# Cross-attention kernel: the normalised context turned by VectorE and put in place by small transfers instead of transposed by TensorE

## What is computed

```
for layer in 1, 2:
    h   = layer_norm(x)
    qh  = (h @ wq + bq) in 16 heads of 128
    kh, vh = (context @ wk + bk), (context @ wv + bv), each with one extra bias row
    ctx = softmax(qh kh^T / sqrt(128)) vh          (per batch and head, over 1501 keys)
    x   = x + ctx @ wo + bo
x = x + gelu(layer_norm(x) @ w_fc1 + b_fc1) @ w_fc2 + b_fc2
```

## Time and profile before

| | us |
|---|---|
| median of 3 runs | 1282.16 |
| lowest, highest of them | 1279.06, 2014.25 |
| the profiled execution, its own time | 1280.71 |
| its span in the trace | 1278.9 |
| mean granted clock of TensorE | 0.996 |

### The profile page before, as it was taken

How to read it: one execution, slowest core, us unless ns; L and a number is a source line. 1 busy time by engine, 2 the same in 40 slices (tenths; PEclk the granted TensorE clock), 3 DMA queues, 4 the chain that set the end, 5 groups by cost and what they waited for, 6 DMA issues and landing times.

```text
span 1278.9 us, 26549 instructions
## 1 busy us (share of the span) xinstructions
PE 1252.2 (98%) x8140; PEld 1152.3 (90%) x8140; DVE 794.6 (62%) x1369; ACT 807.2 (63%) x1585; POOL 905.1 (71%) x750
## 2 busy tenths in 40 slices
PE   6999999999999999999999999999999999999998
PEld 6779999999999999998887999999999999999897
DVE  5745656566666666566785656666656666655654
ACT  4745666666656566676584656666666666666755
POOL 4737777777777777678673768686868686866882
PEclk9999999999999999999999999999999999999999
DMA  5401111111111111012331111111111111101131
GB/s 166 144 10 49 37 61 36 60 36 60 36 60 36 60 37 59 31 39 83 121 126 40 38 38 61 36 60 36 60 36 60 36 60 37 60 30 52 50 95 40
DMA packets 30670, 72.58 MB, mean 57 GB/s; under 512 B 3104, under 2 KB 4512, under 8 KB 30624
## 3 DMA queue, kind: packets, MB, share of 16 engines
q1 hardware_dynamic: 30336, 71.49, 18.1%
q10 hardware_dynamic: 288, 0.52, 0.1%
HBM read 71.52 MB, written 0.48 MB: 56 GB/s over the span
## 4 chain that ended last, share of the span: by engine, by line
PE 91%; DVE 4%; ACT 2%; issue 2%; DMA 0%; POOL 0%; DVEq 0%; ACTq 0%; SPq 0%; POOLq 0%
PE psum L682 36%; PE psum L703 13%; PE psum L704 13%; PE psum L705 13%; PE psum L650 5%; PE psum L747 4%; PE psum L714 2%; PE psum L671 2%; DVE g_prod L1193 1%; PE psum L689 1%; PE psum L696 1%; PE psum L600 1%; DVE qh L1222 1%; ACT on L994 1%; DMA w_raw<-weights 0%
## 5 line engine op out<-in xcount | busy, mean ns | idle before, releaser
L509 POOL TENSOR_TENSOR pt<-slots,pt 125x512 fp32r<-125x512 f32 (+1 forms) x384 | 446.4, 1168 | 216.5 <-ACT slots L988 184.9
L682 PE MATMUL psum<-qs,ctx 128*125 128x384 f32 (+1 forms) x2304 | 543.1, 372 | 1.3 <-ACT slots L1019 0.8
L682 PEld LDWEIGHTS psum<-qs,ctx 128*125 128x125 f32 x2304 | 396.4, 187 | 47.5 <-ACT slots L1019 8.3
L703 PE MATMUL psum<-ctx,pt 125*128 125x258 f32 x1344 | 385.5, 287 | 2.8 <-ACT on L994 2.7
L704 PE MATMUL psum<-ctx,pt 125*128 125x256 f32 x1344 | 379.3, 282 | 0.0
L705 PE MATMUL psum<-ctx,pt 125*128 125x258 f32 x1344 | 379.1, 282 | 0.0
L1281 DVE TENSOR_TENSOR t_max<-psum,t_max 125x512 f32<-125x512 f32 (+1 forms) x320 | 199.2, 622 | 261.2 <-PE psum L682 260.9
L987 ACT ACTIVATE pt<-slots 125x512 fp32r<-125x512 f32 (+1 forms) x384 | 221.1, 576 | 193.1 <-DVE slots L1269 178.6
L1019 ACT ACTIVATE slots<-psum 125x512 f32<-125x512 f32 (+1 forms) x384 | 207.0, 540 | 141.8 <-DVE t_max L1281 132.2
L703 PEld LDWEIGHTS psum<-ctx,pt 125*128 125x128 f32 x1344 | 253.4, 189 | 19.9 <-ACT on L994 12.7
L704 PEld LDWEIGHTS psum<-ctx,pt 125*128 125x128 f32 x1344 | 254.1, 189 | 6.0
(11 more groups left out here) (104 smaller groups left out, 1062.2 us busy)
## 6 DMA issues: line engine op xcount, KB each, us to landing
nat_stage<-ctx_nat SPq DMA_DIRECT2D x64, 375.0 KB
tr_stage<-ctx_tr SPq DMA_DIRECT2D x64, 375.0 KB, 3.0
w_raw<-weights SPq DMA_DIRECT2D x70, 256.0 KB, 2.7
dk_rest<-dk_rows SPq DMA_DIRECT2D x2, 768.0 KB, 6.3
w_raw<-weights ACTq DMA_DIRECT2D x2, 256.0 KB, 4.2
dk_first<-dk_rows SPq DMA_DIRECT2D x2, 256.0 KB, 4.5
xres<-x_rows SPq DMA_DIRECT2D x4, 112.0 KB, 4.3
out_rows<-xres SPq DMA_DIRECT2D x4, 112.0 KB, 1.9
```

Source lines behind the costliest of these rows:

```text
L509: nc.gpsimd.tensor_tensor(split_weights(h, LO, c), slot(h, c), as_f32(split_weights(h, HI, c)), ALU.subtract).then_inc(pt_lo, 1)
L682: last = mm(scores(h, k), ctx_tr_chunk(half, a, c), qs[h][:, m, half, 0:R], start=(half, a, m) == terms[0], stop=(half, a, m) == terms[-1])
L703: mm(out_bank[:, 0:D + 2], hi, ctx_nat_hi(c), start=(c == 0), stop=False, skip_group_check=True)
```

## The change

`on` of a group is no longer transposed by TensorE. VectorE transposes it in blocks of 32 x 32 into a tile `turn` (one instruction a group, at step c = 7). `turn` then holds every block turned in itself, but in the partitions of its rows. 16 DMA transfers a group, one for each pair of a quarter of the rows and a quarter of the dimensions, issued from SyncE's queue, take the blocks to their partitions in `qt`. Each covers 32 partitions and, in each, 8 (h = 0) or 6 (h = 1) runs of 32 elements, 128 bytes. The last group of a layer is still transposed by TensorE.

`qt` is stored by tile: tile, then half, then row. Its readers and writers take the new strides. `turn` lies over `dk_first` and `g_prod`, so the load of `dk_first` for the second layer moves behind the last move of the first layer. `EARLY` is now 49 tiles, so the late copies of heads 0 and 1 cover 7 tiles instead of 3. In SyncE's queue, the moves of a batch's first group stand between tr 0 and nat 1, those of its second group between tr 1 and nat 0; those of the last batch's first group stand behind the first four weight loads of the output stage.

```diff
+QUARTER, QUARTERS = 32, 4
+MOVES = QUARTERS * QUARTERS
+TURNED = GROUPS - 1
+TURN_STEP = 7
+EARLY = NT - TILES
 NAT_W = 2 * D + 2
...
-        qt = sb("qt", [P, DC, B, FLAT], F32)
+        qt = sb("qt", [P, NT, DC, P], F32)
...
+        at_turn = place_at[0]
         dk_first = sb("dk_first", [P, 4 * K], F32)
         g_prod = [sb(f"g_prod{s}", [P, DC, K], F32) for s in range(2)]
+        assert place_at[0] - at_turn == GT[0] * D * 4
...
+        place_at[0] = at_turn
+        turn = sb("turn", [P, GT[0], D], F32)
...
-        qt_flat = qt[:].rearrange("p c b f -> p c (b f)")
+        qt_tiles = qt[:].rearrange("p n c r -> p c n r")
 
         def head_rows_of(h):
 
-            return qt[:].rearrange("p c b (t h e) -> p c (b t) h e", h=H, e=TQ)[:, :, :, ds(h, 1)].rearrange(
+            return qt[:].rearrange("p n c (h e) -> p c n h e", h=H, e=TQ)[:, :, :, ds(h, 1)].rearrange(
                 "p c n a e -> p c n (a e)")
+
+        def of_tiles(ap):
+
+            return ap.rearrange("p (n r) -> p n r", r=P)
 
...
+                def move_context(b, h):
+
+                    sp.wait_ge(turned, INIT + l * TURNED + b * 2 + (h + 1))
+                    settle(sp)
+                    for rows in range(QUARTERS):
+                        for dims in range(QUARTERS):
+                            source = turn[rows * QUARTER:(rows + 1) * QUARTER, 0:GT[h]].rearrange(
+                                "p j (c q r) -> p j c q r", c=DC, q=QUARTERS)[:, :, :, dims].rearrange(
+                                "p j c r -> p (j c) r")
+                            goal = qt[dims * QUARTER:(dims + 1) * QUARTER,
+                                      ds(b * TILES + h * GT[0], GT[h])].rearrange(
+                                "p n c (q r) -> p n c q r", q=QUARTERS)[:, :, :, rows].rearrange(
+                                "p n c r -> p (n c) r")
+                            sp.dma_start(goal, source).then_inc(moved, 16)
+
                 def batch_loads(b, first, last):
 
                     nat, tr = l * (B * PIECES) + b * PIECES, l * (B * PIECES) + b * PIECES + PIECES
                     if not last:
                         load_tr(b + 1, tr, 0)
                     if not first:
+                        move_context(b - 1, 0)
                         for p in range(1, PIECES):
                             load_nat(b, nat + p, p)
                     if not last:
                         load_tr(b + 1, tr + 1, 1)
+                    if not first:
+                        move_context(b - 1, 1)
+                    if not last:
                         load_nat(b + 1, nat + PIECES, 0)
                         for p in range(2, PIECES):
                             load_tr(b + 1, tr + p, p)
 
                 load_bias(l)
-                if l + 1 < LAYERS:
-                    load_dk_first(l + 1)
                 batch_loads(0, True, False)
                 with sp.Fori(1, B - 1) as b:
                     batch_loads(b, False, False)
@@ -423,6 +454,10 @@
                 settle(sp)
                 for u in range(4):
                     load_weight(l * JOBS + (H + u), u, l * H + (H - 3 + u))
+                move_context(B - 1, 0)
+                if l + 1 < LAYERS:
+                    sp.wait_ge(moved, INIT + (l + 1) * (TURNED * MOVES * 16))
+                    load_dk_first(l + 1)
...
-                src = qt_flat[:, half, ds(b * FLAT + h * GT[0] * P, GT[h] * P)]
-                nc.gpsimd.tensor_copy(qs[h][:, HI, half], src).then_inc(qs_hi, 1)
+                src = qt_tiles[:, half, ds(b * TILES + h * GT[0], GT[h])]
+                nc.gpsimd.tensor_copy(of_tiles(qs[h][:, HI, half]), src).then_inc(qs_hi, 1)
                 pool.wait_ge(qs_hi, INIT + n + 1)
                 settle(pool)
-                nc.gpsimd.tensor_tensor(qs[h][:, LO, half], src, as_f32(qs[h][:, HI, half]),
+                nc.gpsimd.tensor_tensor(of_tiles(qs[h][:, LO, half]), src, of_tiles(as_f32(qs[h][:, HI, half])),
...
-                def group_transposes(b, h, pair, out_bank):
-
-                    done = l * GROUPS * 2 + b * 4 + h * 2
-                    if pair == 0:
-                        pe.wait_ge(on_act, INIT + done + 2)
-                        pe.wait_ge(on_dve, INIT + l * (3 * B) + b * 3 + (3 if h else 2))
-                    else:
-                        pe.wait_ge(ot_out, INIT + done + 1)
-                    context_transposes(2 * pair, min(2 * pair + 2, GT[h]), out_bank)
...
-                            pe.wait_ge(ot_out, INIT + group * 2 - 4)
+                            pe.wait_ge(max_ready, INIT + group - 1)
...
-                        if c in (6, 8) and not first:
-                            if c == 6:
-                                pe.wait_ge(max_ready, INIT + group)
-                            group_transposes(b - 1, h, c // 2 - 3, OT_BANK)
...
+                    act.wait_ge(turned, INIT + l * TURNED + b * 2 + h)
...
-                def transposed_context(b, h, pair):
-
-                    j0, j1 = 2 * pair, min(2 * pair + 2, GT[h])
-                    act.wait_ge(ot_mm, INIT + l * (2 * GROUPS) + b * 4 + (2 * h + pair + 1))
-                    go(qt_flat[:, :, ds(b * FLAT + (h * GT[0] + j0) * P, (j1 - j0) * P)],
-                       OT_BANK[:, 0:DC * (j1 - j0) * P].rearrange("p (c r) -> p c r", c=DC),
-                       ACT.Copy).then_inc(ot_out, 1)
...
-                act.wait_ge(ot_out, INIT + (l + 1) * (2 * GROUPS) - 2)
+                act.wait_ge(moved, INIT + ((l + 1) * TURNED - 1) * (MOVES * 16))
                 for s in range(2):
                     go(by_tile(oth[s][:, HI])[:, :, 0:EARLY], head_rows_of(s)[:, :, 0:EARLY],
                        ACT.Copy).then_inc(oth_early, 1)
                 for u in range(1, 4):
                     weight_hi(l * JOBS + (H + u), u, l * 8 + 4)
                 normalized(B - 1, 1, O_LAST)
-                act.wait_ge(ot_mm, INIT + (l + 1) * (2 * GROUPS) - 1)
-                go(qt_flat[:, :, B * FLAT - GT[1] * P:B * FLAT - (GT[1] - 2) * P],
-                   OT_BANK[:, 0:DC * 2 * P].rearrange("p (c r) -> p c r", c=DC), ACT.Copy).then_inc(ot_out, 2)
-                act.wait_ge(ot_out, INIT + (l + 1) * (2 * GROUPS))
+                act.wait_ge(ot_mm, INIT + l * 2 + 1)
+                go(qt_tiles[:, :, NT - GT[1]:NT - 1],
+                   OT_BANK[:, 0:DC * 2 * P].rearrange("p (c n r) -> p c n r", c=DC, r=P), ACT.Copy).then_inc(ot_out, 1)
+                act.wait_ge(ot_out, INIT + l + 1)
                 act.wait_ge(ot_last, INIT + l + 1)
+                act.wait_ge(moved, INIT + (l + 1) * (TURNED * MOVES * 16))
...
-                    dve.wait_ge(ot_mm, INIT + group * 2)
...
+                def turn_context(b, h):
+
+                    dve.wait_ge(on_act, INIT + l * (2 * GROUPS) + b * 4 + (2 * h + 2))
+                    dve.wait_ge(on_dve, INIT + l * (3 * B) + b * 3 + (2 + h))
+                    dve.wait_ge(moved, INIT + (l * TURNED + b * 2 + h) * (MOVES * 16))
+                    V.transpose(turn[:, 0:GT[h]], on[:, 0:GT[h]]).then_inc(turned, 1)
...
+                        if c == TURN_STEP and not first and not (tail and h):
+                            turn_context(b - 1, h)
...
-                dve.wait_ge(ot_mm, INIT + (l + 1) * (2 * GROUPS))
-                V.tensor_copy(qt_flat[:, :, B * FLAT - P:B * FLAT],
-                              OT_LAST[:, 0:DC * P].rearrange("p (c r) -> p c r", c=DC)).then_inc(ot_last, 1)
+                dve.wait_ge(ot_mm, INIT + (l + 1) * 2)
+                V.tensor_copy(qt[:, NT - 1], OT_LAST[:, 0:DC * P].rearrange("p (c r) -> p c r", c=DC)).then_inc(ot_last, 1)
```

More of the change, by code:

```diff
@@ L56 @@
 SPLIT_NEXT, SPLIT_SECOND = (12, 15), (0, 4)
-EARLY = NT - GT[1]
+QUARTER, QUARTERS = 32, 4
[3 more added lines that the diff above has]
+EARLY = NT - TILES
 NAT_W = 2 * D + 2
@@ L237, in build @@
         ot_mm, ot_out, ot_last = sem("ot_mm"), sem("ot_out"), sem("ot_last")
+        turned, moved = sem("turned"), sem("moved")
         pn_picked = sem("pn_picked")
@@ L258, in build @@
                     dv_ready, gp_ready, gp_used, q_lo, first_qs_lo, lb_rows_ready, nat_hi, tr_hi, lb_ready, max_done,
-                    mt_reduced, max_ready, px_ready, sub_done, den_ready, rden_ready, pn_ready, on_dve, ot_last, p80_lo,
+                    mt_reduced, max_ready, px_ready, sub_done, den_ready, rden_ready, pn_ready, on_dve, ot_last, turned, moved, p80_lo,
                     oth_lo, c_lo, xb_ready],
@@ L979, in _ @@
                 for half in range(DC):
-                    go(qs[0][:, HI, half], qt_flat[:, half, 0:GT[0] * P], ACT.Copy).then_inc(first_qs_hi, 1)
+                    go(of_tiles(qs[0][:, HI, half]), qt_tiles[:, half, 0:GT[0]], ACT.Copy).then_inc(first_qs_hi, 1)
                 act.wait_ge(lb_ready, INIT + l + 1)
@@ L1023, in batch_steps @@
                             go(p_extra[:, at], p_extra[:, at], ACT.Exp).then_inc(pe_done, 1)
-                        if c in (6, 8) and not first and not (tail and h == 1):
```

(3 more changed lines are left out.)

## The result

| | before | after |
|---|---|---|
| median, us | 1281.84 (4 runs) | 1306.4 (4 runs) |
| lowest to highest of after, us | | 1304.04 to 1310.74 |
| profiled execution: time, span, us | 1280.71, 1278.9 | 1306.54, 1304.8 |
| mean granted clock of TensorE | 0.996 | 0.986 |

The ratio is 1.0204, with a 95% interval of 1.0178 to 1.0230: the change costs about 25 us. One of the four runs before was a slow one, at 2014.25 us, and isn't in the ratio. I had forecast 1261 us in a range of 1254 to 1286. The result lies outside the range, on the other side of no change.

What follows compares the result with a forecast made beforehand. TensorE, busy for 1252.2 of 1278.9 us, was taken as the bound. 1280.71 less 22.9 for transposes, plus 1.2 for the layers' ends and 1.0 for late loads, gave 1260.0, stated as 1261 for the median; range 1254 to 1286.

Steps and rivals of the forecast that it cites:

- SyncE's issues: SyncE's queue: 16 small transfers a group take 5.8 to 6.9 us to issue, natural piece 1 pushed 0.2 us; cost 0.
- rival A: DMA engines: 128-byte packets take 52 ns each, natural pieces land late and TensorE stalls; 1320 us, chance 0.11.
- air: Score banks ahead of TensorE: a delay under about one step, 2.6 us, isn't seen by TensorE.
- The chain behind it: Moves from 260.0, natural piece 1 landing 5.7 us after issue; a late cast delays VectorE's maximum, ScalarE's copy, then TensorE.
- Packets: DMA engines: 26 ns per 128-byte packet, 6.7 and 5.0 us of each engine a group, no longer than the issue.
- TensorE's saving: TensorE: 212 transposes of 108 ns go, 22.9 us in all, 1.5 us a batch.
- The turn: VectorE's block transpose: 1.5 and 1.1 us a group, cost 0; up to 0.3 us a group at the upper end.
- The layout: New order of qt: only strides change, counted 0; at the upper end 0.1 us a layer on late head copies.
- rival D: ScalarE: with 33 us of work gone, TensorE's waits on `on` halve; 1255 us, chance 0.09.
- Rival C: Moves in SyncE's queue: copies run one after another at 1.9 us each, natural piece 1 very late; 1542 us, chance 0.03.
- The second group: SyncE's queue, a batch's second group: moves out until 298.3, natural piece 0 of the next batch slips 1.5 us; cost 0.
- The layer's end: Tail of the 17 late steps: last move hidden with 4 us of air; the parts together cost +1.2 us.

Runs made afterwards that it cites:

- experiment 2: Changed kernel with all 16 moves a group spread between SyncE's loads (first group: 8 ahead of natural piece 1, 8 behind): 1261.08 us, ratio 0.9845 to the kernel before.
- experiment 4: Changed kernel with 8 moves of 64 partitions a group for 16 of 32, as many packets, half the blocks misplaced: 1259.54 us, ratio 0.9841.
- experiment 7: Changed kernel with only the first group's moves spread around natural piece 1, the second group's 16 in one block: 1259.88 us, ratio 0.9850.
- experiment 1: Changed kernel with all moves left out; turn, layout and order stay: 1259.02 us, ratio 0.9841 to the kernel before.
- experiment 3: Changed kernel with 16 moves a group, each of 2 of 4 tiles or 1 of 3, 3072 packets a batch for 7168: 1299.12 us, ratio 1.0150.
- experiment 8: Changed kernel with neither moves nor VectorE's turn; layout, order and missing transposes stay: 1258.15 us, ratio 0.9832 to the kernel before.
- experiment 6: Kernel before the change plus 16 idle transfers a group of the moves' shape at the moves' queue places: 1349.69 us, ratio 1.0560.

## Why the prediction was wrong, and where it was right

**The step that failed** is "SyncE's issues": "An issue takes 0.43 us (L371) or 0.36 us (L364 at 291.02), so 5.8 to 6.9 us; I take 6.9." It takes 0.608 us and 0.14 us to the next, 11.8 us. I had taken the price from issues of another form (whole tiles, and one outside any loop) and had treated the dearest of these as the upper end, though none was a copy between tiles of SBUF with a pattern of several runs, and though the gap between issues in a loop wasn't in the sum. The text did name "issues stretched well over 0.5 us each, so that SyncE is the late one" as a sign of being wrong, but gave it no price, no rival and no chance. With the measured price the prediction's own chain has the place and most of the lateness: from 260.0 the queue is held until 271.8, the piece lands 5.7 us later at 277.5, 4.1 us after the cast was due. That 271.8 is the point from which rival A was to decide, by another cause. But it doesn't have the time: less the 2.6 us of air this is 14 x 1.5 = 21 us, 1282 us, which is still in the range. Three more terms were short. The moves begin 13.05 us ahead of the cast's due time where I had 13.4, and the load is issued 0.35 us behind their end, so the piece is 4.9 us late in the batch shown, 5.3 at most. The air is smaller (below). And the lowered clock, some 9 us, stands nowhere in the prediction.

**The chain behind it was right.** The turn ended just before the moves began (262.69 and 262.94). Natural piece 1 is the one load whose reader has too little air; its landing was put at 5.7 us and took 5.8. VectorE's stand goes through maximum and copy to TensorE. Experiments 2, 4 and 7 take away that one delay in two ways and get everything back.

**Air** was put at one step, 2.6 us; the table gives 1.6 to 1.9, TensorE's stands 1.9 to 2.0. With 2.6 the measured lateness of 4.92 would have cost 14 x 2.3 = 32 us, where experiment 1 shows 47.

**Packets** were put at 26 ns; they are cheaper. From 234 to 246 us, while a second group's moves run (3072 packets of 128 bytes), q1 has 3390 packets at 25.4% of 16 engines over 12 us. That is 14 ns each on average, and at most 16 for one of the moves'. The queue's line of that stretch:

```profile
q1 hardware_dynamic: 3390, 0.53, 25.4%
```

So rival A had the right place and the right victim, and the wrong cause: I had put all the doubt about the queue into the packets, and experiment 3 finds at most 7 us there. The Trainium skill's 512 bytes ("DMA: Bandwidth & Descriptors", Specifications) don't bound these copies: the 14 ns speak against a doubling, and their landing stays at 1.9 us. The Trainium skill's advice to join many small transfers (same page, Rules for kernel authors) holds here, as experiment 4 shows, but through the issuing queue, not through the DMA engines.

**TensorE's saving** was put at 22.9 us, less some 2 us for tail and loads. Experiments 1, 2 and 8 stand 19 to 22 us below their kernel before. Experiment 2's batch of 61.93 us is the 61.9 predicted.

**The turn** was put at 1.5 and 1.1 us and takes 1.23 and 0.97; hidden, as said. The layout is free within what experiment 8 can tell. ScalarE's relief (rival D) gives nothing beyond the forecast. Rival C, copies one after another, is out: they land in 1.9 us while 16 are issued in 11.8.

**The second group** was put at 0 and is 0, though the transposed piece behind it is 3.1 us late on average and 4.0 at most (43.4 us in 14 waits), which I had not foreseen.

**The layer's end** was put at 1.2 us, with 4 us of air for the last move. In experiment 2 the 16 moves go out from 554.81 to 565.24, the last lands 1.9 us later near 567.1, and the late head copies start at 567.77, behind an evacuation that had waited for TensorE and not for the moves. It is hidden, but with some 0.6 us of air.

Not tried: moves issued from another engine's queue, and fewer than 16 moves that still put every block in its place.

## What to carry to other kernels

A DMA isn't only bytes and packets: its issue holds the queue of the engine that issues it, here 0.6 to 0.75 us each, and everything written behind it in program order waits. Price the issue from a row of the same form (SBUF to SBUF, several runs a partition, in a loop), or bound it well above the dearest row there is. Before a block of small transfers goes into a queue, look for the load behind it whose reader has the least air, and put that load in front of it or in the middle.

## What the runs showed of the hardware that was not expected

- SyncE's time for one issue goes by the form of the pattern, not by the number of packets: 0.29 to 0.36 us for a load of 125 or 128 partitions, 0.53 us for a copy within SBUF of one run a partition, 0.608 us with 2 to 8 runs, 0.613 us for 64 partitions in place of 32.
- A 128-byte packet within SBUF took at most 16 ns of an engine's time.
- After 3.44 us without work TensorE was granted 0.50 from 292 to 296 us in experiment 6 (1.2 of 2.4 GHz) and 1.00 again from 300. In the changed kernel, after 2.96 us without work, it stayed at 1.00 from 284 us on. But the length of the stand doesn't decide: in the batch of experiment 6 from 147.87 us TensorE stood for 3.38 us and the clock was 1.00, and in the changed kernel it fell after 2.84 us (first batch with moves, from 152.65 us) and after 2.33 us (from 848.43 us), by the stretches of that kernel:

```profile
150.00:155.00 5.00, 2.35 (x9) 2.35 (x10) 3.35 (x7) 3.93 (x8) 4.11 (x3) 0.80 0.09 21
155.00:160.00 5.00, 4.82 (x30) 4.49 (x30) 3.40 (x8) 2.36 (x6) 3.19 (x4) 0.86 0.15 58
...
845.00:850.00 5.00, 2.67 (x17) 2.47 (x16) 3.67 (x6) 3.15 (x7) 3.34 (x3) 0.93 0.06 6
850.00:855.00 5.00, 5.00 (x30) 4.82 (x29) 3.22 (x7) 2.26 (x6) 3.97 (x4) 0.73 0.18 71
```

What decides between the two after such like stands was not followed up. The lowered clock comes with the stands: in experiment 2, where TensorE waits at most 0.6 us at a time for ScalarE to free a score bank, the clock of every batch is 1.00.
